# Decoder block on one core: low-rank products in row groups of the array, key-bias products in column groups

## What is computed

```python
w = W(codes, scales) ; y = x @ w.T + (x @ A.T) @ B.T          # low-rank addition, rank 16: q, k, v, o, gate, up, down
w_down = NF4[codes_down] * scales_down + B_down @ A_down      # 512 x 1792, as the kernel folds it
q = h @ Wq.T + bq ; k = ctx @ Wk.T + bk                       # attention over the context, layer 1
p = softmax(q @ k.T / sqrt(512)) ; h = layernorm(h + p @ ctx)
```

## Time and profile before

| what | us |
|---|---|
| median of 3 runs | 739.68 |
| lowest, highest | 739.55, 745.03 |
| profiled execution, its own time | 739.51 |
| span of its profile | 737.7 |
| PE busy in the span | 691.8 |
| DVE, ACT busy | 398.7, 384.4 |

### The profile page before, as it was taken

The page is one execution under the profiler, slowest core; times in us unless marked ns, Lnnn a source line. Parts: engine busy times, 40 slices in busy tenths (PEclk is TensorE's granted clock), DMA queues, the critical chain, the costliest instruction groups (busy, mean ns, idle before and its releaser), DMA issues.

```text
span 737.7 us, 8504 instructions
## 1 busy us (share of the span) xinstructions
PE 691.8 (94%) x3196; PEld 480.7 (65%) x3196; DVE 398.7 (54%) x691; ACT 384.4 (52%) x553; POOL 66.9 (9%) x126
## 2 busy tenths in 40 slices
PE   5879999999999998999999999999997999999993
PEld 3545454544554446888888887888764888887872
DVE  3367776657556773665555623456677222223386
ACT  4456677945557506757575713444434333334653
POOL 1022213201112000000000000002122000000022
PEclk9889999999999799999999999999999999999997
DMA  5582095421123320332423000003450122210002
GB/s 154 200 295 80 3 283 168 135 71 58 61 60 112 92 63 18 107 104 85 122 77 115 5 1 0 1 1 114 157 230 28 58 58 85 66 50 0 0 29 85
DMA packets 24905, 63.32 MB, mean 86 GB/s; under 512 B 5471, under 2 KB 10143, under 8 KB 23970
## 3 DMA queue, kind: packets, MB, share of 16 engines
q1 hardware_dynamic: 24866, 62.79, 26.7%
HBM read 58.06 MB, written 4.72 MB: 85 GB/s over the span
## 4 chain that ended last, share of the span: by engine, by line
PE 84%; DVE 7%; ACT 4%; issue 2%; DMA 2%; POOL 1%; SPq 1%; POOLq 0%; DVEq 0%; ACTq 0%
PE bank L859 16%; PE bank L842 7%; PE bank L843 7%; PE bank L844 7%; PE bank L928 7%; PE bank L929 7%; PE bank L722 4%; PE bank L763 4%; PE bank L652 3%; PE bank L502 2%; PE bank L750 2%; PE bank L845 2%; PE bank L804 2%; PE bank L602 1%; PE bank L578 1%
## 5 line engine op out<-in xcount | busy, mean ns | idle before, releaser
L981 ACT ACTIVATE line<-line 128x1024 f32<-128x1024 f32 x87 | 91.1, 1048 | 0.1
L928 PE MATMUL bank<-xh,wh 128*128 128x512 f32 x224 | 88.4, 395 | 1.5 <-issue 1.5
L859 PE MATMUL bank<-wh,xh 128*128 128x512 f32 x224 | 87.8, 392 | 2.0 <-DVE xl L1689 1.8
L842 PE MATMUL bank<-xh,wh 128*128 128x512 f32 x224 | 87.8, 392 | 1.4 <-DVE th L1637 1.4
L929 PE MATMUL bank<-xl,wh 128*128 128x512 f32 x224 | 88.1, 393 | 0.0
L843 PE MATMUL bank<-xl,wh 128*128 128x512 f32 x224 | 87.5, 391 | 0.0
L859 PE MATMUL bank<-wh,xl 128*128 128x512 f32 x224 | 87.4, 390 | 0.0
L844 PE MATMUL bank<-xh,wl 128*128 128x512 f32 x224 | 87.4, 390 | 0.0
L1332 POOL TENSOR_SCALAR rstd<-mv 128x1 f32<-128x1 f32 x45 | 20.0, 445 | 650.7 <-DVE mv L1703 474.9
L1222 ACT ACTIVATE xh<-arena 128x512 fp32r<-128x512 f32 x56 | 35.4, 632 | 68.5 <-PE bank L859 59.8
L1689 DVE TENSOR_TENSOR xl<-arena,xh 128x512 fp32r<-128x512 f32 x56 | 38.5, 688 | 52.5 <-ACT xh L1222 52.3
(11 more groups left out here) (183 smaller groups left out, 1202.6 us busy)
## 6 DMA issues: line engine op xcount, KB each, us to landing
codes<-in_c_gu SPq DMA_DIRECT2D x14, 512.0 KB, 3.9
scales<-in_s_gu SPq DMA_DIRECT2D x28, 256.0 KB, 3.8
codes<-in_t_gu SPq DMA_DIRECT2D x14, 512.0 KB, 3.6
codes<-in_c_dn SPq DMA_DIRECT2D x7, 512.0 KB, 4.8
scales<-in_s_dn SPq DMA_DIRECT2D x14, 256.0 KB, 3.9
fold<-in_t_dn SPq DMA_DIRECT2D x1, 3584.0 KB, 13.3
codes<-in_c_qkv SPq DMA_DIRECT2D x6, 512.0 KB, 4.9
arena<-in_xT SPq DMA_DIRECT2D x4, 512.0 KB, 4.9
```

Of the source, the lines that this page charges most:

```text
L842: pe.matmul(dst, wh[:, s, c:c + P], xh[:, k, cols], start=(k == 0), stop=False)
L859: last = pe.matmul(bank[b][:, :], h[:, s, b * P:(b + 1) * P], wp[:, s, 0:D], start=first and p == 0, stop=last_one and p == len(parts) - 1)
L928: pe.matmul(dst, wh[:, s, c:c + P], xh[:, k, cols], start=(k == 0), stop=False)
L981: nc.scalar.activation(below(slot), below(slot), ACT.Prelu, bias=bias, scale=scale, alpha=alpha).then_inc(bent, 1)
```

## The change

- `down_lora(j)`: row group j % 3 and column block j // 3; three j to a step in steps 0 to 4 instead of two in steps 0 to 6. PE waits once for three (until all of the three before have been added). DVE adds three in steps 0 to 4. The host lays out `a_d` in the new order.
- `attention_lora(n)`: even n is a part of `wsum` from rows 0 to 63, odd n a part of `woT` from rows 64 to 127 (the rows that were not used are zero); PE waits once for a pair. `lora_l` and `lora_r` are loaded with 128 rows instead of 80.
- `key_step` for the two single rows and `key_bias`: matmul d (or c) writes its own row 32 d of the bank, with no accumulation. ACT copies all 128 partitions of the bank. The four partial rows of the two biases are summed by the next product: `key_columns` uses all 128 rows of `folded` against a column `picked` that is one at rows 0, 32, 64 and 96. The four partial rows of `beta` go to memory as four rows by four DMAs and come back as four; the product with `ones`, now 4 rows, sums them.
- DVE sets up `picked` and clears the constant's column of `wb` at the start, six small memsets more.

```diff
-                    last = pe.matmul(bank[0][0:1, :], k_b[:, d:d + 1], wq1[:, d, :], start=(d == 0), stop=(d == KD - 1))
+                    last = pe.matmul(bank[0][d * ROWG:d * ROWG + 1, :], k_b[:, d:d + 1], wq1[:, d, :], start=True, stop=True)
...
-                        pe.matmul(bank[0][:, n * KD + e:n * KD + e + 1], folded[:, n, e * P:(e + 1) * P], ident[0:1, 0:1], start=True, stop=True)
+                        pe.matmul(bank[0][:, n * KD + e:n * KD + e + 1], folded[:, n, e * P:(e + 1) * P], picked[:, :], start=True, stop=True)
...
-                    last = pe.matmul(bank[7][0:1, :], wb[:, KD + c:KD + c + 1], ctxT[:, g, c, :], start=(c == 0), stop=(c == KD - 1))
+                    last = pe.matmul(bank[7][c * ROWG:c * ROWG + 1, :], wb[:, KD + c:KD + c + 1], ctxT[:, g, c, :], start=True, stop=True)
...
-                if n >= 2:
-                    pe.wait_ge(af_added, n - 1)
-                j = n % KD
-                rows = slice(0, 3 * R1) if n < KD else slice(O_ROW, O_ROW + R1)
+                j, o = divmod(n, 2)
+                if n >= 2 and not o:
+                    pe.wait_ge(af_added, n)
+                rows = slice(o * O_ROW, (o + 1) * O_ROW)
...
-                if j >= 3:
-                    pe.wait_ge(fold_kept, j - 2)
-                rows = slice(QR * (j // DT), QR * (j // DT) + R1)
-                pe.matmul(bank[FOLD_BANK[j % 3]][:, :], a_d[rows, (j % DT) * P:(j % DT + 1) * P], bT_d[rows, :],
+                if j >= 3 and j % 3 == 0:
+                    pe.wait_ge(fold_kept, j)
+                rows = slice(QR * (j % 3), QR * (j % 3) + R1)
+                pe.matmul(bank[FOLD_BANK[j % 3]][:, :], a_d[rows, (j // 3) * P:(j // 3 + 1) * P], bT_d[rows, :],
...
-                for j in range(2 * t, min(2 * t + 2, NF)):
+                for j in range(3 * t, min(3 * t + 3, NF)):
                     down_lora(j)
...
-            sp.dma_start(beta_dram, beta_s).then_inc(kb_out, 16)
+            for c in range(KD):
+                sp.dma_start(beta_dram[c:c + 1, :], beta_s[c * ROWG:c * ROWG + 1, :]).then_inc(kb_out, 16)
...
-                for j in range(2 * b, min(2 * b + 2, NF)):
+                for j in range(3 * b, min(3 * b + 3, NF)):
                     dve.wait_ge(fold_ready, j + 1)
```

More of the change, by code:

```diff
@@ L116, in decoder_kernel @@
     heads_dram = nc.dram_tensor("heads_rows", (P, T), F32, kind="Internal").ap()
-    beta_dram = nc.dram_tensor("beta", (1, T), F32, kind="Internal").ap()
+    beta_dram = nc.dram_tensor("beta", (KD, T), F32, kind="Internal").ap()
     ctx = ExitStack()
@@ L143, in decoder_kernel @@
         al = sb("al", [P, KD, 3 * RG], F32R)
-        with nc.sbuf_tensor("folded", [3 * RG, T], F32) as folded_m:
+        with nc.sbuf_tensor("folded", [P, T], F32) as folded_m:
             pass
-        th = sb("th", [3 * RG, T], F32R)
+        th = sb("th", [P, T], F32R)[0:3 * RG, :]
         ff_s = sb("ff_s", [P, 2, 2])
@@ L199, in decoder_kernel @@
         wk1 = [m[:, 0:D] for m in (bT0, bT_d, a_d, wk3)]
-        lora_l = wo0[0:O_ROW + R1, :]
+        lora_l = wo0
         mT = [wk3, m_free[:, 0:D], m_free[:, D:2 * D], wo0]
@@ L238, in decoder_kernel @@
         lora_r, h_at = carve(heads_m[:, :, :].rearrange("p k t -> p (k t)"), h_at, D)
-        kq_s, lora_r = kq_s.rearrange("p (s t) -> p s t", s=2), lora_r[0:O_ROW + R1, :]
+        kq_s = kq_s.rearrange("p (s t) -> p s t", s=2)
         ctx_h, h_at = carve(heads_m[:, :, :].rearrange("p k t -> p (k t)"), h_at, 5 * D)
         assert h_at <= KD * T
-        beta_s = folded_m[0:1, :]
-        folded = folded_m[0:1, :].rearrange("p (n e) -> p n e", n=2)
+        beta_s = folded_m[:, :]
+        folded = folded_m[:, :].rearrange("p (n e) -> p n e", n=2)
         KQ_F0, CTX_SLOT = NF - 6, NF - 2
@@ L471, in _ @@
                 sp.wait_ge(kq_out[n], 16 * NT // 2)
-            sp.wait_ge(kb_out, 16)
-            for used, dst, src, done in ((KQ_F, kqT, kq_dram, in_kq), (BETA_F, beta[0:1, :], beta_dram, in_kq), (CTX_F, ctx1, i["ctx"], in_ctx1)):
+            sp.wait_ge(kb_out, 16 * KD)
+            for used, dst, src, done in ((KQ_F, kqT, kq_dram, in_kq), (BETA_F, beta[0:KD, :], beta_dram, in_kq), (CTX_F, ctx1, i["ctx"], in_ctx1)):
                 sp.wait_ge(dn_ready, NF + used)
@@ L603, in key_step @@
                 elif c == KD:
-                    last = pe.matmul(bank[0][0:1, :], k_b[:, d:d + 1], wq1[:, d, :], start=(d == 0), stop=(d == KD - 1))
+                    last = pe.matmul(bank[0][d * ROWG:d * ROWG + 1, :], k_b[:, d:d + 1], wq1[:, d, :], start=True, stop=True)
                 else:
-                    last = pe.matmul(bank[0][0:1, :], q_b[:, d:d + 1], wk1[d], start=(d == 0), stop=(d == KD - 1))
+                    last = pe.matmul(bank[0][d * ROWG:d * ROWG + 1, :], q_b[:, d:d + 1], wk1[d], start=True, stop=True)
                 if d == KD - 1:
@@ L898, in x_scores @@
                     pe.matmul(bank[2 + b % 2][:, 0:P], xT[:, k, t], kqT[:, k, t], start=(k == 0), stop=False)
-                pe.matmul(bank[2 + b % 2][:, 0:P], ones[:, :], beta[0:1, t], start=False, stop=True).then_inc(x_ps, 1)
+                pe.matmul(bank[2 + b % 2][:, 0:P], ones[:, :], beta[0:KD, t], start=False, stop=True).then_inc(x_ps, 1)
             def x_probT(b):
@@ L1037, in key_group_out @@
                 else:
-                    nc.scalar.activation(folded[:, c - KD, :], bank[0][0:1, :], ACT.Copy).then_inc(kw_ready, 1)
+                    nc.scalar.activation(folded[:, c - KD, :], bank[0][:, :], ACT.Copy).then_inc(kw_ready, 1)
             def key_columns_out():
@@ L1140, in _ @@
                     act.wait_ge(kb_ps, g + 1)
-                    nc.scalar.activation(beta_s[:, g * 512:(g + 1) * 512], bank[7][0:1, :], ACT.Identity, bias=wb[0:1, 2 * KD:2 * KD + 1]).then_inc(kb_ready, 1)
+                    nc.scalar.activation(beta_s[:, g * 512:(g + 1) * 512], bank[7][:, :], ACT.Identity, bias=wb[:, 2 * KD:2 * KD + 1]).then_inc(kb_ready, 1)
             for t in range(NT + 2):
@@ L1437, in _ @@
             nc.vector.memset(lmT[RMAX:RMAX + 1, :, :], 1.0)
-            link(nc.vector.memset(ones[:, :], 1.0))
+            nc.vector.memset(wb[:, 2 * KD:2 * KD + 1], 0.0)
+            nc.vector.memset(ones[:, :], 1.0)
+            link(nc.vector.memset(picked[:, :], 0.0))
+            for c in range(KD):
+                nc.vector.memset(picked[c * ROWG:c * ROWG + 1, :], 1.0)
             for g in range(HG):
@@ L1568, in add_lora @@
                     dve.wait_ge(scaled, C_DN)
-                dst = wsum[:, n, :] if n < KD else woT[:, n - KD, :]
+                dst = (wsum, woT)[n % 2][:, n // 2, :]
                 nc.vector.tensor_tensor(dst, dst, bank[4 + n % 2][:, :], ALU.add).then_inc(af_added, 1)
@@ L1843, in layout @@
     A, Ba, Bgu = f["L1_attn_lora_A_h"], f["L1_attn_lora_B_attn"], f["L1_attn_lora_B_gu"]
-    lora_l, lora_r = np.zeros((O_ROW + R1, D), np.float32), np.zeros((O_ROW + R1, D), np.float32)
+    lora_l, lora_r = np.zeros((P, D), np.float32), np.zeros((P, D), np.float32)
     lora_l[:3 * R1], lora_r[:3 * R1] = Ba[:3].transpose(0, 2, 1).reshape(3 * R1, D), A[:3].reshape(3 * R1, D)
-    lora_l[O_ROW:], lora_r[O_ROW:] = A[3], Ba[3].T
+    lora_l[O_ROW:O_ROW + R1], lora_r[O_ROW:O_ROW + R1] = A[3], Ba[3].T
     b_gu = np.zeros((NF, 3, 2, R1, 2, P), np.float32)
```

5 lines of the change are left out of this document (3 added, 2 removed).

## The result

The changed kernel takes 721.82 us (median of 4 runs, 719.18 to 723.59), the kernel before, beside it, 740.06. The ratio is 0.974, with a 95% interval of 0.969 to 0.979. The forecast was 723.0 (717 to 730). The profiled execution of the changed kernel took 722.84 us with a span of 721.1, 16.6 less than before.

What follows compares the result with a forecast made beforehand. PE was taken as the bound, 84% of the chain. Gains of 1.0 head, 5.1 context, 3.3 routed, 0.9 clock dip and 6.2 fold sum to 16.5: 739.51 - 16.5 = 723.0 us, range 717 to 730.

Steps and rivals of the forecast that it cites:

- The price of a set: Side-by-side 512-column matmuls: a set of 2, 3 or 4 groups costs two passes, 0.86 us, plus 0.03.
- my schedule: Fold phase step by step at full clock: new PE waits of 2.1, 0.9 and 2.6 us, L813 8.9 us closer.
- halves of 64 rows: Routed phase, L741: halves taken to run together, 3.3 us; rival that they don't, 726.3 us, chance 0.05.
- Head phase: L604 and L606, to 99 us: gains of 0.1 and 0.86, sum 1.0 us; ends 0.1 and 1.7.
- Context phase: L660, 99 to 156 us: two sets gain 2.54 each, 5.1 us, PE stays the bound; ends 4 and 5.2.
- Routed phase: L741, 156 to 226 us: four pairs gain 3.3 us, plus 0.9 for half the clock dip at 179.5.
- Fold phase: L804, 226 to 286 us: 8.9 us gain at full clock, less 2.7 for the clock, 6.2 us.
- I put back 3.4: Fold phase: two thirds of the 5.1 us lost to lower clock assumed to remain; a wait swallows 0.7.
- 6 with two falls: Fold-phase sign: L813 about 9 us closer to the start of L763's phase if the clock holds, 6 with two falls.
- The rest: From 286 us on: phases keep their lengths, gain 0; wrong if one changes by more than 2 us.
- DVE as the bound of the fold phase: Fold-phase rival: DVE's later additions bring back all the sets save; 729.2 us, chance 0.19.

Runs made afterwards that it cites:

- the part alone: Only the attention products in halves of 64 rows, against the kernel before: 731.77 us, ratio 0.989.
- in one group: Changed kernel with all down products reading rows 0 to 15 of the operands, same count, order and waits: 729.65 us, ratio to before 0.986.
- 32 rows: Changed kernel with each down product reading all 32 rows of its group (upper 16 zeros) instead of 16: 721.33 us, ratio to before 0.977.
- additions first with 32 rows: Changed kernel with DVE's three additions ahead of its weight work and 32 rows per down product: 717.11 us, ratio to before 0.969.
- the repeat: The changed kernel run again, unaltered, 723.22 us, beside additions first run again, 715.11 us.
- additions first: Changed kernel with DVE's three additions moved ahead of its weight work in each fold-phase step: 715.10 us, ratio to before 0.969.

## Why the prediction was right

- **The price of a set.** The mechanism is right, the size a little low. Two passes and a stagger: six passes of L806 span 1.13 us with the last pass's 0.59, eight of L662 1.04. From a set's start to the next instruction 1.06 us go by for row groups and 0.97 for column groups, 0.89 said; and L765 behind a set takes 3.63 on the chain, where my schedule had 3.43. For the pairs this cancels, since the pair of before had the same addition (1.91 instead of 1.72). That groups run together was read from L555 and L567, whose passes are a quarter as long; nothing changed with the length. The unseen case, halves of 64 rows, is right too: a pair takes 1.06 of the chain instead of 1.91.
- **Head phase.** 1.0 said, 1.5 measured: L606 and L604 as said; 0.3 of it stands ahead of the edited products (L604 started at 79.31, now at 79.02, as L606), and L617 takes 1.68 on the chain instead of L615's 1.87.
- **Context phase.** 5.1 said and measured. ACT's slack of 3.19 and 3.54 less 2.54 gives 0.65 and 1.00; it is 0.64 and 0.98. The four DMAs and the wider copies cost nothing that shows.
- **Routed phase.** 3.3 for the passes, confirmed by the part alone (3.2). For the lower clock at 179.5 us I took half, 0.9; all of it went, 1.7. Sum 4.2 said, 5.1 measured. Why it went isn't shown: with the attention products alone it went as well, and with it three stretches elsewhere.
- **Fold phase.** The schedule is right and the clock is the term that was mis-sized. Waits of 2.1, 0.9 and 2.6 us were said for the second to fourth set; they are 1.89, none and 2.40 (the lower clock in front of the third set covers its wait, as the text allowed). The gain at full clock was to be 8.9. "I put back 3.4" for the clock failed: 10.2 us ran at half, which costs 5.1, as much as before. The lower clock covers the wait of 0.9, so 4.2 are to be taken off where I took 2.7. That gives 4.7; measured 3.6. The missing 1.1 is the price of the sets: each of the five, with the L765 behind it, takes up to 0.37 us more than my schedule had, some of it hidden by the waits. The sign that I gave for this case ("6 with two falls") missed: two falls came, and L815 starts 3.6 us closer, not 6.
- **The rest** was to stay as it is and gained 1.3: before, the clock was at 0.50 from 572.0 to 575.4, and the changed kernel's profile has no such stretch there. That is chance and not the change: three kernels made from the changed one, with the same code there, have it in their profiles (in one group at 563 us, 32 rows at 558, additions first with 32 rows at 552). The window before:

```profile
572.00:575.40 3.40, 3.40 (x10) 2.62 (x9) 0.75 (x1) 1.15 (x4) 0.00 (x0) 0.50 0.00 0
```

- **The rivals.** DVE as the bound of the fold phase came halfway: it stops PE twice, 4.3 us, but the down products alone still gain 3.3 us. The rule of the Trainium skill in A second HAM failure mode: psum-queue depth-cycling (short idles between groups of matmuls make the clock swing) was the better guide here than my two thirds. The trace agrees with it: both waits, 1.89 and 2.40 us, were followed by a fall, in the repeat too. It isn't the whole of it: a wait of 1.4 us was followed by a fall in one execution and not in another, and with the down products in one group the clock fell behind waits of 0.19 and 0.69.

That the gain of the profiled executions was met to 0.1 us is luck: the fold phase was 2.6 too high, the other four rows 2.7 too low together, and the runs of one kernel differ by 4 us through the clock (the median, 721.82, is 1.2 below the forecast).

## What to carry to other kernels

Products that leave most rows or columns of the array unused can be laid side by side when they are independent, and stand next to each other in PE's list; here the row groups wrote to different banks and the column groups to different partitions of one. Read the price from the distance between starts. Then look at who empties the banks: three results that come at once are three additions that the next set waits for, so these belong ahead of other work on that engine. And multiply the span by the granted clock before comparing kernels, because an idle time of two microseconds on PE can cost as much again behind it (here 3.4 us at half clock behind a wait of 1.89), and because a gain of a few microseconds can be a matter of the clock alone. One profile isn't enough to say where the clock falls: two executions of one kernel differed in it, in the same phase.

## What the runs showed that I had not expected

- More rows, with the same number of passes, made the kernel before 7.4 us faster (740.04 to 732.65), nearly all of it through the clock and 5.1 of it in the fold phase. In the changed kernel 16 to 32 rows made no difference in time that shows, though its stretches were 6.8 us instead of 10.2.
- Changing only the attention products raised the clock of the whole run from 0.971 to 0.978 and gave 8.0 us for 3.2 us of passes. One of the four stretches that went stood behind the changed products. Whether the thicker rows (64 instead of 16 and 48) or the shifted times of other work took them away was not tried separately.
- The changed kernel's new idle time, 4.3 us, cost more than itself: the reordering that removed 2.7 us of it gained 6.7, and in the repeats, where it removed 1.9, it gained 8.1, of which 1.7 lies ahead of the reordered lines.
- The same kernel (additions first) had a stretch at half clock behind its wait of 1.4 us in one profiled execution and none in the other.
